# A decoder layer with 16 experts on one Trainium2 core: expert rows weighted at eviction and added to row sums in memory by the scatter, instead of stored, reloaded, weighted and summed

## What is computed

```python
x = x + attn_ref(layernorm(x))            # linear attention over 16 heads x 64, 128 random features, then FFN 256-1024-256
x = x + xattn_ref(layernorm(x), ctx)      # cross attention: softmax(q k^T / 16) v
x = x + ffn_ref(layernorm(x))             # 16 experts, top 2 of them per token

def ffn_ref(xf, Wg, W1, W2, W3):          # xf: 4096 rows x 256
    probs = softmax(xf @ Wg.T)
    topw, topi = top_k(probs, 2)
    topw = topw / topw.sum(axis=-1, keepdims=True)
    gates = (one_hot(topi, 16) * topw[..., None]).sum(axis=1)
    out = zeros_like(xf)
    for e in range(16):
        h = silu(xf @ W1[e]) * (xf @ W3[e])     # 256 -> 176
        out = out + gates[:, e:e+1] * (h @ W2[e])   # 176 -> 256
    return out
```

## Time and profile before

| | |
|---|---|
| median of 3 runs | 1057.35 us |
| the profiled execution, its own time | 1058.89 us |
| its span | 1057.0 us |
| PE busy | 863.3 us, 82% |
| VectorE (DVE) busy | 622.7 us, 59% |
| GpSimd (POOL) busy | 426.0 us, 40% |
| ScalarE (ACT) busy | 401.5 us, 38% |
| TensorE's granted clock, mean | 0.905 of full |
| memory read / written | 41.02 MB / 19.17 MB |

### The profile page before, as it was taken

How to read it: one execution, slowest core, us unless ns; L and a number is a source line. 1 busy time by engine, 2 the same in 40 slices (tenths; PEclk the granted TensorE clock), 3 DMA queues, 4 the chain that set the end, 5 groups by cost and what they waited for, 6 DMA issues and landing times.

```text
span 1057.0 us, 18754 instructions
## 1 busy us (share of the span) xinstructions
PE 863.3 (82%) x5843; PEld 779.0 (74%) x5844; DVE 622.7 (59%) x1729; ACT 401.5 (38%) x1085; POOL 426.0 (40%) x637
## 2 busy tenths in 40 slices
PE   6899999989999799999999998630768787877730
PEld 6789999988999799999999998620546565655520
DVE  4546767756777467678678666643434343343347
ACT  5146346335355253463364364150123232222210
POOL 4202244342443243443452441533555555555520
PEclk9889999998999899999999999855798989898975
DMA  7000010000001101101100007710222222222259
GB/s 221 1 11 1 31 18 13 30 10 20 30 0 30 30 0 30 29 1 30 30 0 30 21 1 211 160 29 3 70 74 80 77 79 79 73 82 74 80 170 336
DMA packets 48159, 60.59 MB, mean 57 GB/s; under 512 B 7217, under 2 KB 38513, under 8 KB 48129
## 3 DMA queue, kind: packets, MB, share of 16 engines
q1 hardware_dynamic: 34016, 34.93, 11.7%
q0 software_dynamic: 9760, 21.08, 6.5%
q10 hardware_dynamic: 4352, 4.20, 1.1%
HBM read 41.02 MB, written 19.17 MB: 57 GB/s over the span
## 4 chain that ended last, share of the span: by engine, by line
PE 73%; another core or an unknown queue 8%; DMA 6%; DVE 3%; ACT 3%; issue 3%; POOL 2%; SPq 0%; DVEq 0%; ACTq 0%; POOLq 0%
PE ps L626 63%; PE ps L633 4%; PE ps L805 2%; DMA narrow<-expert_rows 2%; PE ps L907 2%; DMA assignments<-assign,place_i 1%; DMA e2b<-in_E 1%; PE ps L893 1%; ACT hidT_hi L948 1%; DVE X L1531 1%; POOL assignments L522 1%; ACT narrow L1140 1%; DVE stat L1184 0%; DMA raw_wT<-in_omegaT 0%
## 5 line engine op out<-in xcount | busy, mean ns | idle before, releaser
L626 PE MATMUL ps<-e_sb,narrow 128*128 x320 | 120.6, 504 | 0.9 <-DVE narrow L1481 0.7
L598 POOL DMA_INDIRECT narrow<-xn_rows,gidx x80 | 76.8, 960 | 90.1 <-DVE gidx L1498 65.4
L468 POOL TENSOR_TENSOR veps<-mv,eps_ln 128x2 f32<-128x2 f32 x48 | 10.8, 226 | 219.2 <-DVE mv L1188 217.8
L604 POOL DMA_INDIRECT expert_rows<-narrow,sidx x80 | 78.6, 983 | 31.8 <-issue 19.7
L626 PE MATMUL ps<-e2a_hi,hidT_hi 128*128 x80 | 43.5, 543 | 58.1 <-ACT hidT_hi L948 57.7
L1493 DVE TENSOR_TENSOR hidT_lo<-ps,hidT_hi 128x256 fp32r<-128x256 f32 x80 | 34.0, 424 | 89.3 <-ACT hidT_hi L948 76.7
L1002 ACT ACTIVATE phi<-ps,nmax 128x128 f32<-128x128 f32 x256 | 71.2, 382 | 21.2 <-DVE nmax L1288 21.2
L626 PE MATMUL ps<-w_hi,fT_hi 128*128 128x256 f32 x256 | 77.5, 303 | 0.7 <-DVE fT_lo L1202 0.7
L522 POOL DMA_INDIRECT assignments<-assign,place_i x64 | 64.0, 1000 | 29.2 <-issue 15.7
L626 PE MATMUL ps<-hT_hi,w_hi 128*128 128x256 f32 x256 | 74.5, 291 | 1.5 <-DVE hT_lo L1202 1.5
L626 PEld LDWEIGHTS ps<-e_sb,narrow 128*128 128x128 f32 x320 | 59.3, 206 | 22.2 <-issue 7.2
(11 more groups left out here) (255 smaller groups left out, 2891.1 us busy)
## 6 DMA issues: line engine op xcount, KB each, us to landing
narrow<-expert_rows SPq DMA_DIRECT2D x16, 512.0 KB, 6.0
e_sb<-in_E SPq DMA_DIRECT2D x4, 1408.0 KB, 12.3
X<-in_x SPq DMA_DIRECT2D x16, 256.0 KB, 3.0
ctx_raw<-in_ctxT SPq DMA_DIRECT2D x16, 256.0 KB, 3.1
xn_rows<-xn SPq DMA_DIRECT2D x16, 256.0 KB
out<-X ACTq DMA_DIRECT2D x16, 256.0 KB, 6.0
raw_w<-in_W SPq DMA_DIRECT2D x2, 1024.0 KB, 7.0
e2a_lo<-in_E SPq DMA_DIRECT2D x1, 2048.0 KB
```

Of the source, the lines that this page charges most:

```text
L598: pool.indirect_dma_start(xg[:, u, :], None, xn3_dram, bass.IndirectOffsetOnAxis(gidx[:, u:u + 1], 0))\
L604: pool.indirect_dma_start(y_dram, bass.IndirectOffsetOnAxis(sidx[:, u:u + 1], 0), yg[:, u, :], None)\
L626: return pe.matmul(out_, lhsT, rhs, start=start, stop=stop)
```

## The change

Each engine's part of it:

- **Gates per sequence.** ACT's exp and three small VectorE operations run in every turn for the sequence r (new function `gates`). `assign` becomes pairs: number and gate. VectorE writes the gate half, so it now waits for `placed` as POOL does, and POOL waits for `gates_ready` before the scatters. An entry of the table is 8 bytes instead of 4; it is cleared with two DMAs instead of one.
- **x2 to memory.** SP stores the x2 rows of the sequence b to `row_sums` in memory in each turn, before the store of xn3 that was there.
- **The plan.** POOL issues eight small DMAs `first_round` (16 x 8 numbers each; their data is not used), one for each `scattered[u]`, so that these semaphores start at 16. The table gather brings twice the columns, TensorE transposes two blocks, and VectorE keeps the gates as `gate_of`, one per slot. `scat_i` is now the token's row. `added_need` holds for each tile two thresholds, for the tile one before and two before: 16 where it belongs to the same expert, else the count at which its scatter has landed.
- **Expert stage.** `rows_out` scales by `gate_of` as it evicts. The scatter adds to `row_sums` in memory (`compute_op=ALU.add`). SP lets the scatters go one by one (`may_add`): tile s when tile s-3 has landed and, by two thresholds that it loads into registers, s-1 and s-2 where they are another expert's. Within an expert a token occurs once, so tiles of one expert never touch the same row.
- **Tail.** No loads, sums and stores. When all scatters have landed, SP and ACT issue eight copies each of 256 KB from `row_sums` to the output.

```diff
-    y_dram = nc.dram_tensor("expert_rows", (NASSIGN + SLOT_TILES * P, D), F32, kind="Internal").ap()
+    sum_dram = nc.dram_tensor("row_sums", (NT * P + SLOT_TILES * P, D), F32, kind="Internal").ap()
...
+    ADDING = 3
...
-        assign = sb("assign", [P, TS * TOPK])
+        assign = sb("assign", [P, TS, TOPK, 2])
...
@@ SP @@
+                    sp.wait_ge(x2_ready, b + 1)
+                    sp.dma_start(sum_v[:, tiles_of(b), :], X[:, tiles_of(b), :]).then_inc(x2_stored, 16)
                     sp.wait_ge(xn3_ready, b + 1)
...
+            def rows_added(s, u):
+                return (s - u) * PER + 16 * 2
+            def slot_tiles(s, u, last):
+                early = s if isinstance(s, int) and s < ADDING else ADDING
+                if early == ADDING:
+                    v = (u - ADDING) % GB
+                    hold(sp, scattered[v], rows_added(s - ADDING, v))
+                near = range(1, min(early, ADDING - 1) + 1)
+                needs = [sp.value_load(added_need[0:1, k - 1, bass.ds(s, 1)], min_val=16,
+                                       max_val=16 * (SLOT_TILES // GB + 1)) for k in near]
+                for k, need in zip(near, needs):
+                    hold(sp, scattered[(u - k) % GB], need)
+                sp.sem_inc(may_add)
+            in_groups(slot_tiles, sp)
...
+            for n in range(0, COPIES, 2):
+                sp.dma_start(out_parts[n], sum_parts[n]).then_inc(out_stored, 16)
...
@@ GpSimd @@
                 hold(pool, assign_ready, r + 1)
+                hold(pool, gates_ready, r + 1)
...
-                                                assign[:, n:n + 1], None).then_inc(placed, 16)
+                                                assign[:, t, j, :], None).then_inc(placed, 16)
...
+            for u in range(GB):
+                pool.dma_start(first_round[:, u, :], x[0, 0:16, u * GB:(u + 1) * GB]).then_inc(scattered[u], 16)
             pool.wait_ge(placed, NSEQ * 16 * TOPK * TS)
...
-                pool.indirect_dma_start(y_dram, bass.IndirectOffsetOnAxis(sidx[:, u:u + 1], 0), yg[:, u, :], None)\
-                    .then_inc(scattered[u], 16)
+                hold(pool, may_add, s + 1)
+                pool.indirect_dma_start(sum_dram, bass.IndirectOffsetOnAxis(sidx[:, u:u + 1], 0), yg[:, u, :], None,
+                                        compute_op=ALU.add).then_inc(scattered[u], 16)
...
@@ ScalarE @@
                     if seq_r is not None:
+                        act.wait_ge(gap_ready, seq_r + 1)
+                        act.activation(egap[:, :], gap[:, :], ACT.Exp).then_inc(egap_ready, 1)
...
-                copy(yg[:, u, :], ps[:, 6 + u % 2, 0:D]).then_inc(yg_ready, 1)
+                act.activation(yg[:, u, :], ps[:, 6 + u % 2, 0:D], ACT.Copy, scale=gate_of[:, bass.ds(s, 1)])\
+                    .then_inc(yg_ready, 1)
...
+            for n in range(1, COPIES, 2):
+                act.dma_start(out_parts[n], sum_parts[n]).then_inc(out_stored, 16)
+            act.wait_ge(out_stored, 16 * COPIES)
...
@@ VectorE @@
+            def gates(r):
...
+                then(dve.tensor_scalar(gden[:, :], egap[:, :], 1.0, None, ALU.add))
+                if not first(r):
+                    hold(dve, placed, r * 16 * TOPK * TS)
+                then(dve.reciprocal(assign[:, :, 0, 1], gden[:, :]))
+                dve.tensor_tensor(assign[:, :, 1, 1], assign[:, :, 0, 1], egap[:, :], ALU.mult)\
+                    .then_inc(gates_ready, 1)
...
+                if r is not None:
+                    dve.wait_ge(egap_ready, r + 1)
+                    gates(r)
...
+            for k in range(1, ADDING):
+                last = dve.scalar_tensor_tensor(added_need[:, k - 1, k:], other_expert[:, k - 1, k:], 16.0,
+                                                round_of[:, 0:SLOT_TILES - k], ALU.mult, ALU.add)
+            then(last)
             dve.wait_ge(table_ps, 1)
+            dve.tensor_copy(gate_of[:, :], ps[:, 2, P:P + SLOT_TILES])
             then(dve.tensor_copy(table[:, :], ps[:, 2, 0:SLOT_TILES]))
```

123 lines of the change are left out of this document (56 added, 67 removed).

## The result

The changed kernel takes **1029.85 us** (median of 4 runs, 1027.27 to 1031.10) beside 1058.04 us for the kernel before (median of 4): ratio 0.971 with a 95% interval of 0.967 to 0.974, 28 us faster. Forecast were 1051 us and a range of 1042 to 1068: the sign was right, the time lies outside the range. Later comparisons, on other chips, added something that no number above shows: on one chip the kernel before takes 975 us, and there variants of the changed kernel are 4% slower than it.

What follows compares the result with a forecast made beforehand. Bounds differ by stage: TensorE in the turns, DMA engines in the tail. 1058.9 + 1.6 + 3.0 + 4.4 + 0.9 - 16.1 = 1052.7 us, 1051.2 against the median; range 1042 to 1068.

Steps and rivals of the forecast that it cites:

- The tail: After the last scatter: 16 memory-to-memory copies, 20 us taken, replace loads, sums and stores; 23.3 us instead of 39.4, 16.1 less.
- The last landing: End of the expert stage: the last adding scatter lands 4.0 instead of 2.40 us after its issue, +1.6 us.
- Rival 1: Expert stage: adding scatters land in say 7 us, the DMA queue becomes the bound, 1078 us; chance 0.17.
- The wait of the gates at `placed`: Turn before the last: VectorE's gate write waits for sequence 13's scatters, delaying prT_lo; +3.0 us, between 0.9 and 4.9.
- first_round: Plan: eight small DMAs on POOL at 1.26 us each delay the table gather, +4.4 us; lower end 0.
- the cover: Plan: 5.95 us from the last assignment scatter's issue end to the table gather, in which POOL's small DMAs could hide.
- The plan as a whole: Plan: +4.4 us for first_round and +0.9 us for the extra transpose, table operations and wider rows.
- the order at the changes of expert: Expert stage: waiting for earlier scatters costs 1.8 us at each of 15 changes, 27 us, hidden by POOL's slack.
- 69 us of POOL's slack: Expert stage: POOL's 117.1 us idle before scatters and gathers, less 47.7 us of fixed gaps; would hide the order's 27 us.
- The turns: Per-sequence turns: added gate operations and x2 stores hide in existing waits, cost 0; without cover 13 turns x 0.8 us.
- Rival 3: Plan: first_round is cheap and sequence 13's scatters land early, so both new costs hide; 1044.7 us, chance 0.20.
- the sum of my most favourable ends: Whole kernel: 12.1 us copy, both plan costs at their lower end, no later landing; 1035 us.

Runs made afterwards that it cites:

- pairs_third: Kernel before with only the table entries widened from 4 to 8 bytes: 1029.5 us against 1058.6 us for the kernel before, ratio 0.974.
- best1_again: Changed kernel with gate operations later on VectorE and first_round DMAs issued ahead of the turns: 1017.3 us, ratio 0.957 to the kernel before.

## Why the prediction came out as it did

By stage, the forecast was +3.0 us to the last `prT_lo`, +5.3 in the plan, +1.6 in the expert stage and -16.1 in the tail; measured were -12.1, -6.8, +13.2 and -22.8. One step failed most: the waits for the table's scatters were priced with the landing times of 4-byte entries, and the earlier trace rows, though the change makes the entries 8 bytes wide, and the turns were put at 0 without a look at what the 4-byte entries do there. With 8-byte entries alone the kernel before gains 29 us on a held chip (pairs_third); beside it, on the same chip, the whole change is only some 2 us faster. So the sign was right in good part by luck: what else the change does (the shorter tail against the longer stage and turns) nearly cancels on a held chip, and on the free chip it makes the kernel slower, as its variants show.

- **The tail** (-16.1 forecast, -22.8 measured). The mis-sized term is the copy. I took 20 us, nearer the end at which memory is touched twice at 347 GB/s; the copies run at 318 GB/s at a DMA share of 0.99, and 4.19 MB at that rate are 13.2 us, near the lower end of 12.1. The Trainium skill (DMA: Bandwidth & Descriptors, Latency and other measured facts) gives 207 to 214 GB/s per direction for copies between tensors in HBM, of tiles whose rows lie 512 KiB or more apart. The trace does not agree for these copies, whose rows lie one behind the other: 318 GB/s, and the measurement decides.
- **The last landing** (+1.6): right. The adding scatter lands in 3.8 us (4.0 taken), 1.4 more than a plain one. Rival 1, an addition that lands in 7 us, fell.
- **The wait of the gates at `placed`** (+3.0): too large. VectorE's timeline of the turn before the last:

```profile
682.71 0.17 DVE L1302 TENSOR_SCALAR gden<-egap 128x2 f32<-128x2 f32 x1 [0.72 <-ACT egap L1093]
683.06 0.17 DVE L1305 RECIPROCAL assign<-gden 128x2 f32<-128x2 f32 x1 [0.19 <-DVE gden L1302]
```

  The reciprocal waits 0.19 us, for its operand: the scatters of sequence 13 had landed at 681.8. The lower end, 0.9 us, was the true value. With 4-byte entries the term would have been about right: in the trace of before the same four landed at 697.7 us, 13.6 us behind the last issue and 2.3 us behind the start of `prT_lo`. With 8 bytes they took 9.25 us and had landed 1.6 us ahead of it.
- **first_round** (+4.4): 2.9 us by best1_again. Eight of these DMAs take 3.96 us, 0.50 each, not 1.26; and the cover, the 5.95 us until the scatters land, shrank to 1.40 by the same oversight. What the prediction took from the Trainium skill (DMA: Bandwidth & Descriptors, Anatomy of one DMA), that few descriptors are issued quickly, is nearer to the trace (0.50 us for 16 rows, 0.96 for 128), though the eight did not hide. The plan as a whole became 6.8 us shorter where 5.3 longer was forecast.
- **The expert stage** (only the last landing forecast, +13.2 in the first measurement). The price of the order at the changes of expert was right, 27 us against 26.4 us of POOL waiting for SP and 27.6 us by experiment. That 69 us of POOL's slack would hide it was wrong: an adding scatter is issued in 1.58 us instead of 0.98, a term that the prediction left out, and this takes 48 us of the slack. POOL then sets the stage (80 x 3.16 = 253 us of the 259.5 without order), so the order costs its 27.6 us in full. That the sum is +13 and not +27 on a held chip has another cause: at POOL's slower pace no tile is late, and the stage without order is 14.6 us shorter than the one before. The slack itself was read from a stage that late tiles had stretched. On the free chip the kernel before has only some 6 us of slack (209 us of stage, 203 of POOL's work), and the addition and the order cost 287 - 209 = 78 us, close to 48 + 27.
- **The turns** (0 forecast, -12.1). Two effects of opposite sign were missed: 0.65 us more in each steady turn, at the sum into X and not at `prT_lo`, where the cover held as forecast, and on held chips alone; and two standstills less, some 20 us, which nothing in the prediction priced. Whoever reads only the clean 100 us of a loop does not see them.
- **Rival 3**, both costs at the plan hidden (1044.7 us), was nearer than the forecast; the sum of my most favourable ends, 1035 us, still missed. The forecast's -6 us is made of -16.1 and +9.9; what came is -22.8, -6.8, -12.1 and +13.2.

## What to carry to other kernels

Price an adding indirect DMA by its issue as well as by its landing: here each row travelled alone, and the queue that issues it had 0.60 us more per 128 rows. Before slack is spent, ask whether the stage that shows it is itself held up, and read the odd iterations of a loop as well as the steady ones. When a change widens or narrows what a DMA carries, price that too: here 8-byte entries in place of 4-byte ones were worth 16 us on one chip and 29 us on another. And time a change on more than one chip before its sign is believed.

## What was not expected of the hardware

- One chip ran the same program 83 us faster than the others (975 against 1058 to 1063 us), 65 us of them in the expert stage. On the others the results of TensorE's matmuls were taken up 3.3 to 3.7 us late in 17 to 20 of 80 tiles where POOL's scatters came as close as 2.56 us, and in none where they were 3.16 us or more apart; TensorE's own pace at the onset was 2.2 us a tile in both. Why those chips do so was not found.
- The profiles of these chips lack records: 702 to 829 of the 1,024 semaphore updates of the table scatters, against 997 to 1,024 on the free chip. A "remote" or a missing landing there may be no more than a lost record; when a dependent instruction starts is the surer sign.
- With scatters of 128 numbers of 4 bytes no semaphore of the core was updated for 5.07 and 5.22 us on such a chip; on the free chip one turn grew by 2.2 us and in another run by 5.7. With 8 bytes no turn grew by more than 0.8 us.
- An indirect DMA on POOL that waits for a memset just ahead of it starts some 0.8 us after the memset's end.
